# Issuing the stores of pruned blocks from ScalarE's DMA queue instead of SyncE's

## The reference

```
edge_feat   = H.T @ V                       # H is adj
att         = softmax(Q @ edge_feat.T * scale * H, axis=1)
comp_mask   = softmax(0.5*structural + 0.5*mean(att)) >= th
cos         = xn @ xn.T                     # normalised, masked nodes
edge_scores = softmax(cos * H, axis=1)
H_pruned    = H * ((edge_scores >= th) & comp_mask[:, None])
connectivity = H_pruned.sum(axis=1);  edeg = H_pruned.sum(axis=0)
agg = H_pruned.T @ (x_final @ W, scaled);  msg = H_pruned @ agg;  out = relu(msg @ Theta)
```

## Time and profile before

| | before |
|---|---|
| median of 3 runs | 2440.88 us (2438.64 to 2444.03) |
| profiled execution | 2440.41 us, span 2438.5 us |
| PE busy | 2055.7 us (84%) |
| DVE busy | 1757.7 us (72%) |
| ACT busy | 779.8 us (32%) |
| DMA, whole span | 834.18 MB, mean 342 GB/s |
| queue q1 (SyncE) | 829.48 MB, 85.0% of the 16 engines |
| queue q10 (ScalarE) | 2.40 MB, 0.3% |
| pruned<-stream, the stores | x64, 2048.0 KB each, median 10.5 us to landing |

### The profile page before, as it was taken

The page is one execution under the profiler, slowest core; times in us unless marked ns, Lnnn a source line. Parts: engine busy times, 40 slices in busy tenths (PEclk is TensorE's granted clock), DMA queues, the critical chain, the costliest instruction groups (busy, mean ns, idle before and its releaser), DMA issues. The chain is left out here.

```text
span 2438.5 us, 36215 instructions
## 1 busy us (share of the span) xinstructions
PE 2055.7 (84%) x15608; PEld 732.7 (30%) x15608; DVE 1757.7 (72%) x2037; ACT 779.8 (32%) x990; POOL 4.5 (0%) x18
## 2 busy tenths in 40 slices
PE   6798959989977766699999989987676689996897
PEld 2224324323221111143344323221111134334333
DVE  7875982268879999965541348879999975553998
ACT  0001000146644333311111036653333311111897
POOL 0000000000000000000000000000000000000000
PEclk9999989999988888899999999988888899997999
DMA  9975989989939999987779989929999987763796
GB/s 385 421 336 233 427 356 425 427 328 376 373 132 424 420 411 410 370 317 277 276 278 386 427 326 376 379 106 411 412 411 410 375 330 270 269 252 156 311 421 253
DMA packets 123486, 834.18 MB, mean 342 GB/s; under 512 B 8512, under 2 KB 10560, under 8 KB 76608
## 3 DMA queue, kind: packets, MB, share of 16 engines
q1 hardware_dynamic: 121136, 829.48, 85.0%
q10 hardware_dynamic: 2192, 2.40, 0.3%
HBM read 695.54 MB, written 136.31 MB: 341 GB/s over the span
## 5 line engine op out<-in xcount | busy, mean ns | idle before, releaser
L923 ACT ACTIVATE stream<-stream,negmax 128x4096 f32<-128x4096 f32 x128 | 475.2, 3713 | 521.4 <-DVE negmax L917 521.4
L912 DVE CUSTOM_DVE_ANT_0 stream<-ps,stream 128x1024 f32<-128x1024 f32 x352 | 413.9, 1220 | 55.3 <-PE ps L876 31.9
L876 PE MATMUL ps<-edgeT,node_twice 64*128 64x512 f32 x1024 | 281.0, 669 | 183.5 <-DVE mx L912 183.4
L455 PE MATMUL ps<-stream,stage 128*64 128x512 f32 x1728 | 387.8, 600 | 42.8 <-DMA stream<-in_adjT 27.4
L876 PE MATMUL ps<-edgeT,query_twice 64*128 64x512 f32 x1024 | 249.6, 619 | 6.3 <-DVE edgeT L944 4.0
L1209 PE MATMUL ps<-stream,xw 32*64 32x512 f32 x4096 | 230.5, 595 | 3.7 <-issue 3.0
L455 PEld LDWEIGHTS ps<-stream,stage 128*64 128x64 f32 x1728 | 122.1, 138 | 300.6 <-issue 221.5
L876 PEld LDWEIGHTS ps<-edgeT,node_twice 64*128 64x128 f32 x1024 | 94.2, 201 | 377.9 <-DVE mx L912 267.6
L894 PE MATMUL ps<-stream,ones 128*1 128x512 f32 x1024 | 185.4, 862 | 11.1 <-DVE stream L1249 11.1
L1249 DVE SCALAR_TENSOR_TENSOR stream<-stream,cut 128x4096 f32<-128x4096 f32 x40 | 179.4, 4484 | 1.4
L1427 DVE SCALAR_TENSOR_TENSOR query_twice<-stream,query_twice 128x512 bf16<-128x512 f32 x256 | 154.7, 679 | 4.6 <-ACT query_twice L1405 4.5
(11 more groups left out here) (195 smaller groups left out, 1692.9 us busy)
## 6 DMA issues: line engine op xcount, KB each, us to landing
stream<-in_adj SPq DMA_DIRECT2D x136, 2048.0 KB, 13.0
stream<-in_adjT SPq DMA_DIRECT2D x74, 2048.0 KB, 13.2
pruned<-stream SPq DMA_DIRECT2D x64, 2048.0 KB, 10.5
spare<-in_adj SPq DMA_DIRECT2D x26, 2048.0 KB, 10.3
spare<-pruned SPq DMA_DIRECT2D x22, 2048.0 KB, 11.5
query_twice<-pruned SPq DMA_DIRECT2D x22, 2048.0 KB, 11.3
node_twice<-pruned SPq DMA_DIRECT2D x20, 2048.0 KB, 11.5
query_twice<-in_adj SPq DMA_DIRECT2D x14, 2048.0 KB, 15.7
```

The lines of the kernel that those rows point to most:

```text
L455: last = nc.tensor.matmul(ps[F * h:F * h + F, bank + b, :], stage[:, t.k % SL, :], half_bank(src, b, h), start=False, stop=False, skip_gro ...
L876: last = nc.tensor.matmul(ps[:, 2 * slot + h, :], stationary[F * h:F * h + F, rows_n], bank_of(edgeT[F * h:F * h + F, :], c), start=True, ...
L912: nc.vector.tensor_tensor_reduce(out=prod[s][:, cols], in0=ps[:, 2 * slot:2 * slot + 2, :].rearrange("p a b -> p (a b)"), in1=block_in[:, ...
L923: nc.scalar.activation(prod[s], prod[s], ACT.Exp, bias=negmax[:, s:s + 1], accum_out=zsum[:, s:s + 1]).then_inc(exp_done, 1)
```

## The change

SyncE no longer issues the stores; it issues load(n+5) by itself when P(n) has passed. ScalarE issues store(n-1) after the exponential of block n, with its own wait on `pruned`; the last store follows at the end. The rolled loop of exponentials becomes 32 exponentials in line. Buffers, semaphores and the waits on them are as they were.

```
-                R, LEAD = 4, 11
+                R = 4
...
                     for n in range(NB):
                         sp.wait_ge(pruned, n + 1)
-                        sp.dma_start(Hp[seq[n]], prod[n % SL3]).then_inc(stored[n % SL3], 16)
                         if n + HELD < NB:
                             load(n + HELD)
...
                 @block.scalar
                 def _(act):
-                    row_blocks(act, 3, LEAD, lambda t: exponentials(act, t, max_ready, exp_done), seq)
+                    def store(n):
+                        act.wait_ge(pruned, n + 1)
+                        act.dma_start(Hp[seq[n]], prod[n % SL3]).then_inc(stored[n % SL3], 16)
+
+                    for n in range(NB):
+                        exponentials(act, last_step(n, seq), max_ready, exp_done)
+                        if n >= 1:
+                            store(n - 1)
+                    store(NB - 1)
```

## The result

The change makes the kernel slower: 2535.36 us (median of 4 runs, 2527.51 to 2538.75) against 2439.95 us before, ratio 1.0386 with a 95% interval of 1.0366 to 1.0405. I had forecast slower, because VectorE would wait longer for its stores, but 2480 us with a range up to 2500.

What follows compares the result with a forecast made beforehand. It took VectorE's waits for stores to land, beside nearly full DMA engines, as the bound. The profiled 2440.4 us plus 40.1 (21.0 + 19.1) for slower landings, other terms zero, gave 2480.5, stated as 2480; range 2453 to 2500.

Steps and rivals of the forecast that it cites:

- what bounds the kernel: Prune phase: VectorE (93% busy) and DMA engines (share 1.00) nearly full; VectorE's 14.9 us of gaps are waits for stores.
- T = (L + 9.73)/2: Prune phase: period per block from a two-block loop of store landing and VectorE work, unless VectorE alone sets it.
- L: A store's time from issue to landing in the prune phase: median 10.5 us before, forecast 12.0 us after.
- packets one to one, no more bandwidth from a second queue: Prune-phase DMA: store and load queues alternate packets; the sum is no larger, 416 GB/s together against 414 for one.
- Rival A: Prune phase: stores in effect served ahead of loads, landing in 7.2 us; faster, 2425 us; chance 9%.
- ScalarE's wait: Added wait before ScalarE's store issue: about 0.35 us lies in a 5 us gap before the next exponential; cost 0.
- SyncE's issues: SyncE loses 64 issues of 0.33 us, loads start up to 0.37 us earlier; not felt, 0.
- the rolled loop: ScalarE's rolled loop of exponentials goes; ScalarE idles 162.6 us there, so 0.
- (a): Prune phase, store and load in different queues: landing 12.0 us, period 10.87 us, cost 21.0 + 19.1 = 40.1 us.
- the 7.2 of a store that I took for undisturbed: Store(0), which found the queue empty: 7.2 us to landing, 5.05 us DMA time plus 2.15 us fixed time.
- (e): End of the prune phase, after place 26, where no loads remain: no cost, between -2 and +2 us.
- C: Prune phase: a store's queue starts late behind packets already taken on; landing 14.2 us, much slower, 2538 us; chance 6%.

Runs made afterwards that it cites:

- k = 4: Changed kernel, but SyncE issues load(n+5) only after ws(n+2) has read all four of its chunks: 2486.15 us, ratio 1.0175.
- k = 1: Changed kernel, but SyncE issues load(n+5) only after ws(n+2) has read one of its four chunks: 2448.16 us, ratio 1.0032.

## Why the prediction was wrong

**Right: what bounds the kernel.** VectorE's loop over a store's landing, T = (L + 9.73)/2, holds. With the mean landing of each pass (14.1 and 14.0) it gives 11.9 us for the changed kernel; the periods seen are 11.86 and 11.79. With half a load it gives 10.1, with the late loads 10.6 (k = 4) and 10.1 (k = 1), 0.1 to 0.4 us under the periods seen. With a fourth buffer, which takes the loop away, the loss goes with it.

**Right: packets one to one, no more bandwidth from a second queue.** 3710 beside 3696. The Trainium skill, "DMA: Bandwidth & Descriptors", section "Queues, rings and completion order", has an engine drain a whole packet of some 9 to 17 descriptors before it turns to another queue. In this trace a transfer's eight did not go as one piece: from 783 to 784 us 14 profile packets of each queue ran on the 16 engines, and no store landed ahead of its load. Rival A is dead.

**Right: the terms at zero for ScalarE's wait, SyncE's issues and the rolled loop.** The run with everything in ScalarE's queue is at 0.9999. ScalarE's issue took 0.36 us.

**Wrong: the size of L in (a), 12.0 us.** This is the step that failed. The landing measured 14.4 in the median and 14.1 in the mean, so 26 periods cost 90.2 us in the two passes instead of 40.1. With 14.1 the same sum gives 309.8 us per pass, 94.7 for both, 2535 in all: nothing but L was off by much.

I had built L from a fixed part, the 7.2 of a store that I took for undisturbed, and 5.05 us of load, the DMA time of a transfer in a full queue, as if the 16 engines ended together. They do not. A store's semaphore rises by one when an engine is through with its share, and the landing is the sixteenth step. The traces hold the times of the steps. Medians of the transfers issued from 722 to 985 us, in us from the issue:

| run, transfer | 8th engine | 16th engine, the landing |
|---|---|---|
| before, store | 7.1 | 10.5 |
| after, store | 12.4 | 14.4 |
| load first in one queue, store | 12.8 | 14.8 |
| half of the load, store | 9.7 | 10.3 |
| no loads, store | 6.2 | 6.3 |
| no stores, load | 7.2 | 8.2 |

So there are two errors in L, one for the middle engine and one for the last.

- **The middle engine** ended at 12.4, beside the 12.25 of my sum, but partly by luck. A store by itself is 6.2 and not 7.2, and the load beside it costs 6.2 and not 5.05. A load that finds the engines idle starts slowly (0.96 us more per engine, above), and the change lets the queues run dry in each period, which I had written down ("the DMA engines idle 0.8 us per block") and not priced. The row for it, a load of 8.2 us at 692 us, was in the trace of before.
- **The last engine** ended 2 us behind the middle one. I had moved L "nearer to the first, since the landing waits for the slowest of 16 engines", and allowed nothing for how far behind the slowest is. In the mean over both passes the middle engine ended at 12.6, 0.6 us over my 12.0, and the last 1.5 us behind it. At half a us per period and us, over 52 periods, the first is worth 16 us and the second 39: with the 40 forecast they make the 94.7. With half a load, 2.7 of the 4.1 us that the landing fell came off the middle engine and the rest off the last one's delay.

That 6.3 for a store alone and 8.1 for a load alone add up to the 14.4 is chance. Both hold the time outside the transfer itself (6.3 less 4.9 of DMA time, 1.4 us), and a pair has it once.

I had also misread the kernel before. "It waits 10.5 - 7.2 = 3.3 us for the load ahead" is not so for most engines: the eighth is through at 7.1 us there, 0.9 behind a store by itself, and only the last few make the landing 10.5.

**What makes the last engine late.** In the run without loads it goes with a packet of the instruction queue, seven times out of seven. In the changed kernel 13 of the 54 stores from place 0 to 26 have such a packet in their time, and in all 13 the last engine is 1.8 to 2.7 us behind the eighth. Of the other 41 some end together (0.2 us) and some do not (up to 2.9), with runs of late ones behind each other. A late engine can hand its delay on: the store issued at 767.94 landed at 782.3, 2.3 us after the next pair was issued. How much of the rest that explains was not tried; nor was a run without instruction fetches.

**Wrong: (e), the end of the phase at zero.** Same cause: ws(29) waits for store(26), the last that has a load beside it. It landed in 14.6 and 15.3 us where the sum had 12.0, 2.6 and 3.3 more; measured +2.6 and +3.7.

**The rivals.** C came out at the measured time, 2538 us with L = 14.2, but by a different reason, so this is luck. It had the store wait behind packets that a deep load queue had taken on, and the queue is not deep here. What is common to both is that a store's first packet stands behind a load's. In rival A a sum is off by half a us: 56 transfers at 5.05 and the fixed 2.15 are 285.0, not 285.5.

That reads on idle engines start slowly is shown; what in the memory makes them slow is not.

## What to carry to other kernels

Before a transfer is moved to another queue, ask whether its landing is waited for, and what then runs beside it. A time to landing is valid only for the state of the queue in which it was read; if the change lets the queues run dry, price the transfers from rows of transfers that started on idle engines. A landing is the end of the slowest of the engines: see how far it is behind the others before a sum is built on it. If a landing is on the path, one more buffer for it was worth more here (2426 to 2433 us) than any order of issues (2441.59 at best).

## What the runs showed of the hardware

- A 2 MB store to device memory that finds the 16 engines idle lands in 6.3 us, a 2 MB load in 8.1 to 8.4; in a full queue either takes 4.9 to 5.05 us of DMA time. About 1 us of the difference is at the load's start, where the engines move 164 to 262 GB/s, and the rest is that the engines of a load end further apart (7.2 and 8.2 us for the 8th and the 16th, against 6.2 and 6.3).
- The same load, started 1.2 to 4.3 us behind a store in another queue, shows hardly any slow start, and 87 of 95 us come back.
- A store alone with an instruction fetch in its time landed in 8.2 to 8.6 us instead of 6.3, seven times out of seven.
- Two full queues, one reading and one writing, move 418 to 422 GB/s, one alone 414 to 419.
